# Last two passes of a gated cross-attention and mixture-of-experts kernel: the products for the output projection are made two in a slot, the matmuls of the group before fill the softmax, and five products of the last group stand in PSUM banks

## The reference, cut to what matters

```python
x = x + tanh(g_xattn) * cross_attention(context, layernorm(x))   # softmax over 77 context rows
h = layernorm(x)
# the second half, per token n:
w = softmax over the chosen experts of (normalised h @ normalised sim_matrix - sigmoid(gates))
q = sum_e w[n,e] * (h @ q_proj[e]);  k, v likewise                # 16 experts, all computed
attn = softmax(q k^T / sqrt(128)) inside each sequence
o = attn @ v
out = sum_e (w[n,e] * o[n]) @ o_proj[e]
x = x + tanh(g_ffn) * out
```

## Time and profile before

| | before |
|---|---|
| median of 3 runs | 880.05 us |
| the profiled execution: its time | 878.19 us |
| its span, first to last instruction | 876.4 us |
| PE busy, share of the span | 94% |
| VectorE (DVE), ScalarE (ACT), GpSimd (POOL) busy | 71%, 59%, 63% |
| mean granted TensorE clock | 0.997 |

### The profile page before, as it was taken

One profiled execution on the slowest core, in us unless ns is written; L12 is line 12 of the kernel. 1 busy time (PEld: TensorE's weight loads), 2 busy tenths in 40 slices (PEclk: granted clock), 3 DMA queues, 4 the chain that ended last, 5 costly groups with the idle time before them and its releaser, 6 DMA issues.

```text
span 876.4 us, 16223 instructions
## 1 busy us (share of the span) xinstructions
PE 822.3 (94%) x4344; PEld 458.2 (52%) x4344; DVE 618.1 (71%) x1575; ACT 518.2 (59%) x1148; POOL 550.7 (63%) x588
## 2 busy tenths in 40 slices
PE   4579999999999999999999999999999999999974
PEld 3445555555555555555555555555555555545431
DVE  3777577777686867768686776868677686876545
ACT  3555657565665756566575656657575565656353
POOL 2265567576685857567585756759475765857464
PEclk9999999999999999999999999999999999999999
DMA  8753655453654645364564536465463636546342
GB/s 223 193 193 106 192 176 189 139 200 130 219 160 166 209 156 191 111 227 151 186 210 153 192 108 218 145 205 191 152 212 111 226 111 210 185 182 217 93 159 72
DMA packets 58531, 150.49 MB, mean 172 GB/s; under 512 B 5568, under 2 KB 22144, under 8 KB 58496
## 3 DMA queue, kind: packets, MB, share of 16 engines
q1 hardware_dynamic: 57776, 150.00, 51.8%
q10 hardware_dynamic: 720, 0.08, 0.1%
HBM read 145.34 MB, written 4.72 MB: 171 GB/s over the span
## 4 chain that ended last, share of the span: by engine, by line
PE 80%; DVE 6%; ACT 5%; issue 4%; POOL 2%; DMA 1%; ACTq 1%; DVEq 0%; POOLq 0%
PE acc_v L893 17%; PE acc_k L893 17%; PE acc_q L893 16%; PE acc_o L909 16%; DVE zo_full L756 2%; ACT pc L550 2%; PE m L1032 2%; PE m L960 2%; PE m L931 2%; POOL stage L460 2%; PE oT_p L985 2%; PE m L1014 1%; PE m L923 1%; PE m L1001 1%; DVE zq_full L746 1%
## 5 line engine op out<-in xcount | busy, mean ns | idle before, releaser
L455 POOL TENSOR_TENSOR zq<-zq_full,zq 128x512 f16<-128x512 f32 x192 | 224.6, 1171 | 201.0 <-ACT zq L508 200.9
L460 POOL TENSOR_TENSOR stage<-zo_full,stage 128x512 f16<-128x512 f32 x208 | 239.4, 1160 | 69.7 <-ACT stage L516 69.7
L508 ACT ACTIVATE zq<-zq_full 128x512 f16<-128x512 f32 x256 | 161.1, 630 | 203.6 <-DVE zq_full L746 199.2
L909 PE MATMUL acc_o<-stage,w_hi 128*128 128x512 f16 x512 | 193.5, 381 | 10.3 <-POOL stage L460 7.3
L746 DVE TENSOR_TENSOR zq_full<-wq_bc,x2T_p 128x512 f32<-128x512 f32 x256 | 172.9, 677 | 35.1 <-ACT x2T_p L609 26.5
L893 PE MATMUL acc_q<-zq,w_hi 128*128 128x512 f16 x512 | 194.7, 380 | 0.0
L893 PE MATMUL acc_k<-zq,w_hi 128*128 128x512 f16 x512 | 194.5, 380 | 0.0
L893 PE MATMUL acc_v<-zq,w_hi 128*128 128x512 f16 x512 | 194.5, 380 | 0.0
L756 DVE TENSOR_TENSOR zo_full<-stage,oT_p 128x512 f32<-128x512 f32 x256 | 169.9, 677 | 6.5 <-PE oT_p L985 5.9
L516 ACT ACTIVATE stage<-zo_full 128x512 f16<-128x512 f32 x256 | 158.2, 629 | 25.7 <-DVE zo_full L756 25.1
L909 PE MATMUL acc_o<-stage,w_lo 128*128 128x512 f16 x256 | 97.5, 381 | 0.0
(11 more groups left out here) (141 smaller groups left out, 1067.6 us busy)
## 6 DMA issues: line engine op xcount, KB each, us to landing
wq_bc<-w_rows SPq DMA_DIRECT2D x128, 512.0 KB, 5.0
stage<-w_rows SPq DMA_DIRECT2D x128, 512.0 KB, 4.0
out_dram<-x_all SPq DMA_DIRECT2D x16, 256.0 KB, 4.3
ctx_g<-in_ctx_dram SPq DMA_DIRECT2D x16, 154.0 KB
x_all<-in_x_dram SPq DMA_DIRECT2D x2, 256.0 KB, 6.7
x_all<-in_x_dram SPq DMA_DIRECT2D x1, 512.0 KB, 9.2
w_rows<-wT SPq DMA_DIRECT2D x16, 32.0 KB, 3.2
wq_sb<-in_L_xattn_Wq_dram SPq DMA_DIRECT2D x1, 64.0 KB, 5.5
```

The lines of the kernel that those rows point to most:

```text
L455: nc.gpsimd.tensor_tensor(zq[:, 1, e % Z_SLOTS, :], zq_full[:, e % F_SLOTS, :], zq[:, 0, e % Z_SLOTS, :], ALU.subtract).then_inc(zq_lo_poo ...
L460: nc.gpsimd.tensor_tensor(zo[:, 1, e % Z_SLOTS, :], zo_full[:, e % F_SLOTS, :], zo[:, 0, e % Z_SLOTS, :], ALU.subtract).then_inc(zo_lo_poo ...
L508: nc.scalar.activation(zq[:, 0, e % Z_SLOTS, :], zq_full[:, e % F_SLOTS, :], ACT.Copy).then_inc(zq_hi_done, 1)
L909: last = nc.tensor.matmul(acc[O][:], w[:, O, e, :], zo[:, half, e % Z_SLOTS, :], start=(e == 0 and n == 0), stop=(e == E - 1 and n == 2))
```

## The change

It touches passes 15, 16 and 17 alone.

- Pass 15 makes 12 products of group 14 in place of 8: experts 0 to 7 two in a slot in slots 8 to 11, then 8 to 11 one in a slot. Pass 16 makes 12 to 15 of group 14 in slots 0, 1 and 3, and from slot 8 on all 16 products of group 15, two in a slot. Pass 17 makes none. The loads of the gate weights move with them (slots 1, 3, 5, 7 and 8 to 11).
- TensorE's order in pass 16: scores of group 15 first, then the v transposes, then output experts 5 to 13 of group 14, the transposes of the probabilities, experts 14 and 15, oT, the transposes of outT of group 14, and from slot 8 the 16 experts of group 15. outT of group 14 goes on ScalarE from slot 10 to 5, its sum into `x_all` on VectorE from slot 12 to 8.
- For group 15 VectorE makes the low halves of experts 1, 4, 7, 10, 13 (O_LOW_DVE_LAST), one slot after the product. The float32 products of these five stand in the PSUM banks `acc_q`, `acc_k`, `acc_v`, `x2T_p` and again `acc_q`. The other eleven take the four slots of `zo_full` by turns.

The diff, cut to its core:

```diff
+O_LOW_DVE_LAST = (1, 4, 7, 10, 13)
         def zo_at(i, s):
+            if isinstance(i, int) and i >= NG - 1:
+                return [(NG - 3 + k, e) for k, e in END_MADE[i - NG + 1].get(s, ())]
+        TWO = {s: tuple((2, 2 * (s - 8) + k) for k in range(2)) for s in range(8, E)}
+        FILL = {8: (0, 1), 9: (2, 3), 10: (4, 5), 11: (6, 7), 12: (8,), 13: (9,), 14: (10,), 15: (11,)}
+        END_MADE = [{s: tuple((0, e) for e in O_LATE.get(s, ())) + tuple((1, e) for e in FILL.get(s, ()))
+                     for s in range(E)}, {0: ((1, 12),), 1: ((1, 13),), 3: ((1, 14), (1, 15)), **TWO}, {}]
         def out_at(i, s):
+            if isinstance(i, int) and i >= NG:
+                return [(i - 1, 2 * (s - 8) + k) for k in range(2)] if s >= 8 and i == NG else []
...
+        END_BANKS = [acc[Q], acc[K], acc[V], x2T_p]
+        END_POOL = [e for e in range(E) if e not in O_LOW_DVE_LAST]
+        def zo_product(g, e):
+            if not is_last(g):
+                return zo_full[:, e % F_SLOTS, :]
+            if e in O_LOW_DVE_LAST:
+                return END_BANKS[O_LOW_DVE_LAST.index(e) % len(END_BANKS)][:]
+            return zo_full[:, END_POOL.index(e) % F_SLOTS, :]
+        def wait_zo_room(eng, g, e):
+            if not is_last(g):
+                wait_zo_low(eng, *before(g, e, F_SLOTS))
+            elif e in O_LOW_DVE_LAST:
+                n = O_LOW_DVE_LAST.index(e)
+                if n >= len(END_BANKS):
+                    wait_zo_low(eng, g, O_LOW_DVE_LAST[n - len(END_BANKS)])
+                elif n < 3:
+                    eng.wait_ge(acc_sb[n], NG)
+            else:
+                n = END_POOL.index(e)
+                if n < F_SLOTS:
+                    wait_zo_low(eng, g - 1, E - F_SLOTS + n)
+                else:
+                    wait_zo_low(eng, g, END_POOL[n - F_SLOTS])
...
 # SyncE
-                    if s % 2 == 1:
+                    if isinstance(i, int) and i >= NG - 1:
+                        if s in (1, 3, 5, 7) or 8 <= s < 12:
+                            spread_o(gc, s // 2 if s < 8 else s - 4)
+                    elif s % 2 == 1:
 # ScalarE: outT
-                    if s == 10 and has(gd):
+                    if s == (5 if is_last(gd + 1) else 10) and has(gd):
 # VectorE: the sum into x_all, and the low halves at the end of a slot
-                    if s == 12 and has(gd):
+                    if s == (8 if is_last(gd + 1) else 12) and has(gd):
-                    for g, e in zo_at(i, s):
-                        if e in O_LOW_DVE:
+                    for g, e in zo_at(i, s - 1 if isinstance(i, int) and i == NG else s):
+                        if e in zo_low_dve(g):
 # TensorE
+                    end = isinstance(i, int) and i == NG
+                    if s == 0 and end:
+                        scores(gc, i)
                     if s == 0 and has(gc):
                         ... v transposes ...
+                    if end and s < 2:
+                        for e in (range(E - O_FIRST, 12), (12, 13))[s]:
+                            out_expert(gd, e)
-                    if s == 1 and has(gc):
+                    if s == 1 and has(gc) and not end:
+                        scores(gc, i)
                     if s == 4 and has(gc):
                         ... transposes of the probabilities ...
+                        if end:
+                            out_expert(gd, 14)
+                            out_expert(gd, 15)
-                    if s == 12 and has(gd):
+                    if s == (7 if is_last(gd + 1) else 12) and has(gd):
```

## The result

| | before | after |
|---|---|---|
| median of the first runs | 880.17 us (4 runs) | 867.76 us (867.29 to 868.15, 4 runs) |
| ratio, 95% interval | | 0.9859 (0.9844 to 0.9874) |
| profiled execution: time, span | 878.19, 876.4 | 867.71, 865.9 |

The change makes the kernel 1.4% faster: 12.4 us by these medians. The forecast was 869.0 us, 11.0 less than before. The 95% interval of the ratio allows 11.1 to 13.7 us. The spans of the two profiled executions differ by 10.5.

A forecast was written before the change was run, and what follows sets the result against it. The prediction took TensorE's waits at the end as the room to gain, with VectorE bounding the last group. 1.6 us before oT and 9.4 behind it give -11.0, from the median 880.05 to 869.0 us, range 867 to 873.

The forecast's parts named there:

- Pass 15 at no cost: Pass 15: four more products don't delay TensorE; low halves of zq end by 827.1, so 3.7 us remain.
- To oT: Pass 16 from 833.40: the exp stall goes, TensorE's own queue sets the pace, oT at 842.30, -1.58 us.
- Against the median: End time: sum gives 867.2 against the profiled execution; the median lies 1.9 higher, so the forecast is 869.0 us.
- a rival for the last group: TensorE's clock falls to 1.2 GHz in the last group: time 872.0 us, chance 12%.
- VectorE as the bound of the last group: Last group: VectorE sets the pace to product 15, 12.77 us of products, low halves, sums and scaling.
- Costs that no row shows: VectorE's products into PSUM (taken as 0, -0.1 to +0.5) and low halves from PSUM (undisturbed, far end +3.9 us).
- (1): Last group: GpSimd slows VectorE's low halves from PSUM too, price 2.1 us, time 871.1, chance 12%.
- (2): Last group: TensorE's clock falls, costing 3 us if the last experts fall into it, time 872.0, chance 12%.
- (3): Last group: a load of gate weights lands late, 0.5 to 1.6 us, time 870.0, chance 14%.
- (4): Pass 15: extra products starve the q, k, v matmuls, price 13 us, time 882, chance 3%.
- (5): Last group: products wait in the new order, only the exp's stall goes, 1.6 us gained, time 878.5, chance 4%.

The follow-up runs named there:

- the longer rounds: The changed kernel once more, no edit, beside the kernel before on the same chip: 867.8 us against 879.66, ratio 0.9871.
- the second profile of before: The kernel before, unchanged, profiled once more: median 879.85 us, ratio 1.0005; this profiled execution took 879.77, span 878.0.
- the second profile of the changed kernel: Profile from the repeat of the changed kernel, no edit: median 867.8 us against 879.66 for the kernel before, span 865.8.

## Why the prediction was right, and where it was off

| step | predicted | profile after | less the 0.29 us that pass 16 starts later |
|---|---|---|---|
| pass 16 starts | 833.40 | 833.69 | 833.40 |
| transposes of the probabilities | 840.56 | 840.85 | 840.56 |
| oT | 842.30 | 842.58 | 842.29 |
| product 0 | 843.39 | 843.67 | 843.38 |
| product 15 | 856.16 | 856.67 | 856.38 |
| last low half ends | 859.24 | 859.76 | 859.47 |
| span | 865.4 | 865.9 | 865.6 |

- **Pass 15 at no cost**: right. The last low half of zq ended at 825.84, later than before and within the 827.1 given; TensorE was busy 13.00 of 13.00 us.
- **To oT**: the chain was right to 0.01 us once the start is taken out, and the stall is gone. One time inside it was too short, without effect: the row maxima and the scaling took 1.96 us (834.78 to 836.74) and not 1.0, the exp began 0.3 us later than forecast, and there were 2.5 us to spare. The prediction doesn't separate two causes that the runs do: the early products bring oT forward, and TensorE's new order makes the sum of group 14 ready in time.
- **Against the median**: this step was off. It carried the 1.9 us by which the median of before lay over its profiled execution (880.05 - 878.19) into the forecast. After the change there is no such distance (867.71 against a median of 867.76), so the profiled times are met to 0.5 us (867.2 against 867.71), and the medians only to 1.2 (869.0 against 867.8). The forecast of -11.0 lies in the interval of the longer rounds (10.0 to 12.7 us) and just outside that of the first (11.1 to 13.7). The two errors point in opposite directions: 0.5 us too much gain in the trace, 0.9 to 1.4 too little between the medians.
- **The clock before**: the sum took the 2.79 us stall from an execution in which the clock stayed up behind it, and priced the removal at -1.58. In the second profile of before the clock fell there, for 1.4 us more, and filling the stall gained 1.1 us by the medians. The same event was weighed as a rival for the last group and not as a cost that before may already pay. This can be the reason why the median of before lies above its first profile and that of the changed kernel doesn't. It is argued from two profiles, and the spread of before isn't settled.
- **VectorE as the bound of the last group**: right. Taking the sum off its way gained 1.1 us (1.0 with the loads early), and removing a load's wait from it 0.5. Two terms were off and partly cancel: the sums cost 1.04 to the next product and not 1.23 (the scaling of rs_d no longer stands behind them), and the load for product 12 cost 0.38 and not 0. It fell at the product whose margin was given as 4.9 us; landing took up to 5.5 us after the change, more than the 5.0 of the earlier trace rows. Four loads are issued there within 5.2 us, which may be why. The wait isn't constant: 0.24 us in the second profile of the changed kernel, 0.73 with the matmuls before expert 0.
- **Costs that no row shows**: both zero, as taken. A product written to PSUM takes 0.68 to 0.69; the low half from PSUM is undisturbed. That the memory is the reason was tested by moving the five products to SBUF: +1.6 us.
- **Rivals**: (1) fell by the rows (its price had a slip, 4 x 0.5 is 2.0 and not 2.1). (2) happened, 0.50 from 847 to 850, and cost nothing that the times show: experts 1 and 2 ran slowly, TensorE caught up, and keeping the clock up gained nothing. (3) happened at 0.38 to 0.5 us, at or under the low end of its price. (4) and (5) fell.

## What to carry to other kernels

Where an engine in order sets the pace of a tail, look at what stands in its queue that nobody behind it needs yet: moving the sum behind the last product gained 1.1 us (0.4 in the profiled execution, where the loads took back the rest), and the loads and the split of the low halves had to follow for the next 0.8. Give VectorE an input in PSUM where GpSimd works beside it on SBUF. Look at what stands ahead of the softmax on ScalarE: two high halves that waited for their products held up the exp. And price a stall of TensorE in more than one execution: in two profiles its length was the same (2.79 and 2.80 us), the clock behind it was not.

## What the runs showed of the hardware

- The same 2.8 us idle time of TensorE was followed by 1.2 GHz in one execution of the kernel before and by 2.4 GHz in another, a difference of 1.4 us. Filling it with matmuls that nothing reads gained 1.1 us by the medians; that all of it comes from this fall of the clock isn't shown.
- VectorE and GpSimd, both reading two tiles in SBUF, delay each other in both directions: 1.48 in place of 0.68 us on VectorE, up to 1.61 in place of 1.15 us on GpSimd. With one input of VectorE in PSUM neither shows it (0.68 us, and 1.15 to 1.17 for each of GpSimd's eleven).
- VectorE reading one bank and writing another (acc_q from oT_p) takes 0.69 us, as into SBUF.
